# Projections and attention in one block: the first quad's loads and first max tiles between the last batch's projection groups

## What is computed

```python
x = x + tanh(g_xattn[0]) * attention(layernorm(x), ctx, mask, mask, Wq, bq, Wk, bk, Wv, bv)
x = x + tanh(g_ffn[0]) * ffn_fp8(layernorm(x), W2, scale, scale1)
# attention: q = Wq x + bq; k = Wk c + bk; v = Wv c + bv, 16 heads of 32 channels
#   dot = mask * (q k / sqrt(32)) - (1 - mask) * 1e6 ; out = (softmax(dot) * mask) v
```

## Time and profile before

| | us |
|---|---|
| median of 3 runs | 2610.9 (2610.55 to 2611.96) |
| the profiled execution | 2608.16 |
| its span in the trace | 2606.3 |
| PE busy in the span | 2505.3 (96%) |
| DVE busy | 1978.2 (76%) |
| POOL busy | 1653.4 (63%) |
| ACT busy | 1393.0 (53%) |

### The profile page before, as it was taken

The page is one execution under the profiler, slowest core; times in us unless marked ns, Lnnn a source line. Parts: engine busy times, 40 slices in busy tenths (PEclk is TensorE's granted clock), DMA queues, the critical chain, the costliest instruction groups (busy, mean ns, idle before and its releaser), DMA issues.

```text
span 2606.3 us, 40566 instructions
## 1 busy us (share of the span) xinstructions
PE 2505.3 (96%) x13169; PEld 1385.0 (53%) x13169; DVE 1978.2 (76%) x3251; ACT 1393.0 (53%) x2606; POOL 1653.4 (63%) x1265
## 2 busy tenths in 40 slices
PE   5999999978999999999999999999999999999995
PEld 4888888864444444444444444444444444444441
DVE  5766666637788888888888888888888888888863
ACT  2333333322666666666666666666666666666662
POOL 1333333422777777777777777777777777777774
PEclk8999999996999999999999999999999999999997
DMA  6666666655334444444444444344444444444411
GB/s 213 229 236 236 234 234 233 237 171 96 76 80 89 88 96 91 98 103 99 103 98 93 91 93 93 88 88 88 96 91 96 102 100 102 100 94 92 91 37 49
DMA packets 242040, 314.48 MB, mean 121 GB/s; under 512 B 75033, under 2 KB 142681, under 8 KB 241857
## 3 DMA queue, kind: packets, MB, share of 16 engines
q1 hardware_dynamic: 229712, 274.20, 42.2%
q10 hardware_dynamic: 12144, 38.02, 4.1%
HBM read 200.09 MB, written 102.11 MB: 116 GB/s over the span
## 4 chain that ended last, share of the span: by engine, by line
PE 66%; DVE 6%; issue 3%; POOL 1%; DMA 1%; ACT 0%; SPq 0%; DVEq 0%; POOLq 0%; ACTq 0%
PE s_bank L690 19%; PE o_bank L716 18%; PE x_bank L703 16%; PE d_bank L727 7%; PE x_bank L742 5%; DVE part_max L849 4%; POOL pair_sum L942 1%; PE x_bank L734 1%; DVE y L103 1%; DMA q_st<-qx_scr 0%; DVE isnan L102 0%; POOL y L951 0%; ACT probs L785 0%; DMA inv_b<-inv_scr 0%; DVE neg_max L863 0%
## 5 line engine op out<-in xcount | busy, mean ns | idle before, releaser
L942 POOL TENSOR_TENSOR pair_sum<-probs 128x512 f32<-128x512 f32 x1024 | 1284.2, 1288 | 472.0 <-ACT probs L785 472.0
L849 DVE TENSOR_REDUCE part_max<-x_bank 128x1 f32<-128x512 f32 x2048 | 1280.9, 683 | 355.6 <-PE x_bank L703 348.8
L785 ACT ACTIVATE probs<-s_bank 128x512 f32<-128x512 f32 x2048 | 1071.5, 604 | 662.3 <-PE s_bank L690 655.0
L690 PE MATMUL s_bank<-q_st,k_st 100*128 100x512 f32 x2048 | 876.5, 430 | 4.7 <-ACT probs L785 4.7
L703 PE MATMUL x_bank<-k_st,q_st 98*128 98x512 f32 x2048 | 823.6, 406 | 24.8 <-DMA q_st<-qx_scr 21.5
L690 PEld LDWEIGHTS s_bank<-q_st,k_st 100*128 100x128 f32 x2048 | 387.1, 189 | 511.5 <-issue 263.2
L716 PE MATMUL o_bank<-probs,v_t 128*32 128x512 f32 x4096 | 545.5, 605 | 0.0
L703 PEld LDWEIGHTS x_bank<-k_st,q_st 98*128 98x128 f32 x2048 | 393.1, 192 | 141.8 <-DMA q_st<-qx_scr 22.0
L727 PE MATMUL d_bank<-pair_sum,ones 128*32 128x512 f32 x2048 | 266.6, 592 | 2.8 <-POOL pair_sum L942 2.8
L322 POOL TENSOR_TENSOR stage_lo<-stage,stage_hi 128x512 fp32r<-128x512 f32 x128 | 187.3, 1487 | 120.7 <-ACT stage_hi L392 120.1
L392 ACT ACTIVATE stage_hi<-stage 128x512 fp32r<-128x512 f32 x128 | 79.8, 632 | 190.2 <-DVE stage L476 142.9
(11 more groups left out here) (96 smaller groups left out, 2018.9 us busy)
## 6 DMA issues: line engine op xcount, KB each, us to landing
k_st<-k_scr SPq DMA_DIRECT2D x96, 512.0 KB
q_st<-q_scr SPq DMA_DIRECT2D x192, 256.0 KB
c_raw<-in_ctx_dram ACTq DMA_DIRECT2D x32, 512.0 KB, 6.7
x_raw<-in_x_dram ACTq DMA_DIRECT2D x32, 512.0 KB, 6.2
k_scr<-stage_hi SPq DMA_DIRECT2D x64, 256.0 KB, 2.4
k_scr<-stage_lo SPq DMA_DIRECT2D x64, 256.0 KB, 2.6
v_scr<-stage SPq DMA_DIRECT2D x64, 256.0 KB, 2.7
q_scr<-stage_hi SPq DMA_DIRECT2D x64, 256.0 KB, 2.1
```

Source lines behind the costliest of these rows:

```text
L690: nc.tensor.matmul(s_bank_of(n, k)[:, :], k_st[p][0:KS, h, j * P:(j + 1) * P], q_st[p][0:KS, th, h, :], start=True, stop=True).then_inc(sc ...
L785: nc.scalar.activation(probs[:, c % PR, h, :], s_bank_of(n, k)[:, :], ACT.Exp).then_inc(exp_done, 1)
L849: nc.vector.tensor_reduce(part_max[:, th, sh, at:at + 1], x_bank_of(n, "tile", k)[:, :], AX, ALU.max).then_inc(max_done, 2)
L942: nc.gpsimd.tensor_tensor(pair_sum[:, r % 2, h], probs[:, a, h], probs[:, a + 1, h], ALU.add).then_inc(pair_done, 1)
```

## The change

The projections and the attention become one block. All PSUM is one set of eight banks: attention's s banks are banks 0 to 2, o and d are 3 and 4, x are 5 to 7. Small tiles and the stage buffers get places of their own; `k_st[0]` and `q_st[0]` lie where `c_raw` and `x_raw` were, and `k_st[1]`, `q_st[1]` over the projection weights.

- Only in the last batch, PE's groups go round five banks (0 to 4), so group g waits for group g - 5.
- SP issues `stack_k(0, 0)` at the start of the last batch, after `clo_done`; `stack_q(0, 0)` before the stores of group 4, after `xlo_done`; `load_v(0, 0)` before those of group 16; `set_max(0, 0, 0)` before those of group 20; and `stack_k(1, 1)`, `stack_q(1, 1)` before those of group 22, after the last group is done.
- From group 12 PE runs one slot of period -1 after each group's four channel blocks: slots 19 to 63, which hold the 45 max tiles of quad 0 and one turn of the maxima. DVE takes three maxima, evacuates the group, takes the fourth.
- DVE's last `round_w2` moves from between v groups 11 and 12 to before v group 8.
- The unused `ident_b` and its copy go; the semaphore waits at the block's end go, and `wait_stored` has SP wait for a batch's stores at each fourth quad.

```diff
+            G_MAX = 12
+            def slots_of_group(g):
+                first = XLEAD + 4 * (g - G_MAX)
+                return range(first, min(first + 4, NSLOT)) if g >= G_MAX else range(0)
+            def bank_of_group(g, more):
+                return bank[g % NB] if more else bank[g % NB_LAST]
...
 # SP
                     def batch(b, more):
+                        if not more:
+                            sp.wait_ge(clo_done, B * CB)
+                            stack_k(0, 0)
                         for g in range(G):
+                            if not more and g == 4:
+                                sp.wait_ge(xlo_done, B * CB)
+                                stack_q(0, 0)
+                            if not more and g == GK + GV:
+                                sp.wait_ge(w2_done, B)
+                                load_v(0, 0)
+                            if not more and g == G - 4:
+                                set_max(0, 0, 0)
+                            if not more and g == G - 2:
+                                sp.wait_ge(group_done, B * G)
+                                stack_k(1, 1)
+                                stack_q(1, 1)
...
 # PE
+                            back = NB if more or g < NB_LAST else NB_LAST
+                            if counted(b * G + g + 1 - back):
+                                pe.wait_ge(evacuated, b * G + g + 1 - back)
...
+                                if not more and cb < len(slots_of_group(g)):
+                                    slot(-1, 1, slots_of_group(g)[cb])
...
 # DVE
+                        for g in range(GK // 2, GK + GV // 2 if more else GK):
+                            evacuate(b, g, more)
+                        round_w2(b)
+                        if more:
...
+                        else:
+                            for g in range(GK, GK + GV):
+                                max_and_evacuate(b, g)
...
+                    def max_and_evacuate(b, g):
+                        slots = slots_of_group(g)
+                        for k in slots[:CB - 1]:
+                            slot(-1, 1, k)
+                        evacuate(b, g, False)
+                        for k in slots[CB - 1:]:
+                            slot(-1, 1, k)
...
-                for n in range(-2, NQ + 2):
+                for n in range(NQ + 2):
```

More of the change, by code:

```diff
@@ new lines, in flamingo_gated_layer @@
+        inv_c = sb("inv_c", [P, HALF // 32], F32)
+        tm_c = sb("tm_c", [P, TH, HALF // 32], F32)
+        st2 = sb("st2", [P, 2, 6], F32)
+        mv2 = sb("mv2", [P, 2], F32)
+        ve2 = sb("ve2", [P, 1], F32)
+        rs2 = sb("rs2", [P, 1], F32)
+        rss = sb("rss", [P, 2], F32)
+        nb2 = sb("nb2", [P, 1], F32)
+        bank = [pb(f"bank{i}", [P, HALF], F32) for i in range(8)]
+        c_loaded = [sem(f"c_loaded{i}") for i in range(CB)]
+        x_loaded = [sem(f"x_loaded{i}") for i in range(CB)]
@@ L118, in flamingo_gated_layer @@
-            x_raw = sb("x_raw", [P, CB, T], F32, st)
-            c_loaded = [sem(f"c_loaded{i}", st) for i in range(CB)]
-            x_loaded = [sem(f"x_loaded{i}", st) for i in range(CB)]
             with ExitStack() as su:
@@ L606, in flamingo_gated_layer @@
[L606 to L613 removed]
+            v_t = [sb(f"v_t{i}", [P, SJ, P], F32, at) for i in range(2)]
+            s_bank, o_bank, d_bank, x_bank = bank[0:3], bank[3], bank[4], bank[5:8]
@@ new lines, in flamingo_gated_layer, with run_batches @@
+            NB, NB_LAST = len(bank), 5
+            GK = CB * 2
+            GV = SJ
+            G = 2 * GK + GV
+            G_MAX = 12
[4 more added lines that the diff above has]
+                return bank[g % NB] if more else bank[g % NB_LAST]
+            def run_batches(eng, batch):
+                batch(0, True)
+                if B > 2:
+                    with eng.Fori(1, B - 1) as b:
+                        batch(b, True)
+                batch(B - 1, False)
@@ L1080 @@
+                            slot(n, p, k)
+                    low_ctx(0)
+                    statistics(0)
+                    normalize(0)
+                    run_batches(dve, batch)
+                    run_periods(period)
 _INS = ['x', 'ctx_2048', 'mask_Bx1x2048_fk1', 'g_xattn', 'g_ffn', 'L0_xattn_Wq', 'L0_xattn_bq', 'L0_xattn_Wk',
```

1044 lines of the change are left out of this document (508 added, 536 removed).

## The result

| | before | changed |
|---|---|---|
| median of 4 runs each, one chip, us | 2611.43 (2610.55 to 2612.59) | 2564.81 (2563.17 to 2569.08) |
| ratio, 95% interval | | 0.9824 (0.9807 to 0.9841) |
| the profiled execution, us | 2608.16 | 2563.17 |
| its span, us | 2606.3 | 2561.4 |

The changed kernel is 46.6 us faster. The forecast was 36.2 us, and the time lies 3.2 us under the low end of the range.

The account below looks back on a forecast made before the run. PE, 96% busy, bounds the kernel; gains lie in the 50.6 us gap. With waits of 3.0 and 2.5 us, slot 19 moves from 638.92 to 602.75, 36.2 us less: 2610.9 to 2574.7 us, range 2568 to 2586.

Parts of the forecast that it names:

- the first sentence of the new timeline: Seven batches before the last: same instructions, so the last batch's first matmul stays at 506.82, a change of 0.
- the rival on the new places: Attention: new banks and SBUF addresses stretch PE's steady pace, paid 32 times; then, say, 2618 us; chance 0.05.
- the gap closes: Between projections and scores: the 50.6 us gap goes, 45 max tiles cost 10.6 us among the projections, first score near 587.
- the queue: SP's queue, last batch: stack loads delay stores, DVE stands 4.3 us at `evacuate(12)`, PE loses 3.0 us (bounds 0 to 8).
- the first rival: SP's queue: loads hold stores longer, `evacuate(12)` stalls over 8 us and the clock falls; 2582 to 2596 us, chance 0.11.
- the forecast's own case: Whole run: 0 to 8 us for the queue, 0 to 5 for quad 1; 2569 to 2582 us, chance 0.72.
- quad 1's stack: Slot 19, after the first score: stack issued at 584.25, tile 0 can start at 599.75, PE waits 2.5 us.
- DVE has room: Last batch's groups: four maxima and one evacuation take 3.1 us of a 3.7 us group, 0.6 us to spare.
- The rounding of W2: DVE, last batch: 6.0 us, moved before group 8, about 529.7 to 535.7, costing nothing.
- attention keeps its pace: Attention behind the gap: unchanged, with PE at least 61.3 us busy in 62 us stretches.

Follow-up runs that it names:

- lay_only_c: The kernel before with y8 copied plainly, not transposed, and the projections' SBUF tiles at the changed kernel's offsets; schedule as before: 2598.9 us, ratio 0.9954.
- after_pad64_c: The changed kernel with y8 copied plainly, not transposed, and 64 bytes of padding between weights and split inputs (and ahead of `v_t`): 2570.6 us.
- before_c: The kernel before with one edit, the transposing transfer of y8 made a plain copy of the same size: 2609.86 us, ratio 0.9994.
- after_c: The changed kernel with one edit, the transposing transfer of y8 made a plain copy: 2565.39 us, ratio 0.9823.
- late_half_c: From after_c, the second half of quad 0's q stack is issued before group 16 instead of group 4: 2557.6 us, ratio 0.9798.

## Why the prediction was wrong, point by point

**The step that failed** is the first sentence of the new timeline: "The first matmul of the last batch stays at 506.82: the seven batches before are the same instructions." It came at 498.71. The instructions are the same, their operands' addresses are not, and `lay_only_c` shows that these alone give it. The change moves every tile of the projections, and the diff says so; the text took from that only a rival by which new places might slow attention. The projections' pitch of 0.230 was taken as what the engine does with 512 columns, and the rival on the new places even leaned on it ("at one pace of 0.230 us"). It is a mean of two paces, 0.229 for q and 0.233 for v, and that groups of one shape differ was the sign, readable before, that something beside the shape sets it. This term was 0 and should have been -8.1 between these two traces. With attention's 3.7 us, whose cause is open, it carries the time out of the range.

**Right: the gap closes.** The first score follows the last projection at its pitch, the clock no longer falls at the end of the projections, and the 45 max tiles ride along. The stretch took 83.16 us where 80.4 were forecast. At about the pace that the forecast was made for, `after_pad64_c` has 80.9, in one run.

**Right in place, undersized: the queue.** The wait is DVE's at group 12, ended by a v store, with the loads in order ahead of it. DVE waits 4.66 us (forecast 4.3), PE 4.23 (forecast 3.0), and 1.5 us go to the clock. At the old pace it was 2.67 and 2.4 (`after_pad64_c`), without the clock: what this term is over the forecast comes from the pace again, and the forecast was somewhat high for its own pace. That the two nearly meet at 4.3 and 4.66 us is luck. The mechanism of the first rival, a pause that takes the clock down, came true within the forecast's own case: a pause of 4.2 us was enough, where the text charged it only from 8.

**Right: quad 1's stack.** From the first score to its first max tile 15.55 us, as forecast (599.75 - 584.2), with 1.75 us of waiting instead of 2.5.

**Right: DVE has room.** Beside the pause, PE waits for a maximum once more before 620, for 0.3 us. The rounding of W2 took longer than the 6.0 us that were charged. Its steps on DVE's timeline of the changed kernel, and POOL beside them:

```profile
524.83 2.20 DVE L98 TENSOR_TENSOR w2q<-w2f,w2big 128x1024 bf16<-128x1024 f32 x1
527.06 1.40 DVE L101 TENSOR_SCALAR w2nan<-w2q 128x1024 bf16<-128x1024 bf16 x1
528.50 1.66 DVE L102 TENSOR_TENSOR w2q<-w2q,w2nan 128x1024 bf16<-128x1024 bf16 x1
...
523.68 7.63 POOL L469 TENSOR_TENSOR stage_lo<-stage,stage_hi 128x512 fp32r<-128x512 f32 x4 [6.31 <-ACT stage_hi L697]
```

The same three steps took 1.22, 0.43 and 0.69 us before, when POOL was idle, and they take 1.23, 0.43 and 0.69 in the changed kernel one batch earlier (470.57 to 472.99), where POOL is idle too. In the last batch POOL subtracts beside them, and the whole takes 8.9 us. It stayed under cover. The Trainium skill, page "SBUF — State Buffer", section "SBUF: two separate sides", names the port that GpSimd and the vector engine share as the place where compute engines meet; the two batches fit that. But the port itself shows in no trace, and no run here took POOL's work away from these steps, so this cause is argued and not shown.

**Nearly right: attention keeps its pace.** Forecast as unchanged, it is 3.7 us or 0.2% shorter over 31 quads, too little to be seen in stretches of 62 us. Two of them, of the changed kernel (before: the earlier trace rows, 61.35 and 61.66):

```profile
840.00:902.00 62.00, 61.50 (x348) 29.57 (x347) 50.96 (x89) 38.31 (x76) 46.34 (x37) 1.00 0.43 96
2300.00:2362.00 62.00, 61.67 (x344) 29.96 (x342) 50.93 (x88) 38.50 (x76) 46.34 (x37) 1.00 0.42 93
```

`k_st` and `q_st` have a distance of 0 modulo 256 bytes in both kernels, which fits.

The profiled execution in one line: forecast 2572.0, minus 8.1 for the addresses, plus 2.8 for the last batch (1.2 more pause, 1.5 clock, 0.1 of small terms), minus 3.7 for attention and plus 0.3 around it, gives 2563.3; measured 2563.17. Without the addresses and attention's 3.7 us the step from the forecast to the measurement would be 3 us, and inside the range.

## What to carry to other kernels

A change that moves tiles changes the pace of code that it doesn't touch: before "the same instructions take the same time", compare the addresses of stationary and moving operands, and if two kinds of matmul of one shape have two pitches, try a padding first. It is one line, and here it is worth 10 us (2599 to 2600 instead of 2610). A load that nobody needs for 20 us should not stand in a queue ahead of a store that frees a buffer: give it a later place or another queue. And where one engine gets faster, work out again the waits that are set by transfers, since those grow by what it gained.

## What the runs showed of the hardware

- An fp32r matmul of 512 columns with its own weight load takes 0.2267 us from start to start where both operands lie alike modulo 256 bytes in a partition, and 0.229 to 0.233 us where they lie 64 or 128 bytes apart; at 64 the pace changes from group to group at the same addresses (21.97 or 22.40 us for 96 in `before_c`).
- Three steps of DVE on 128x1024 took 2.20, 1.40 and 1.66 us beside POOL's subtractions and 1.23, 0.43 and 0.69 us without them, in one trace (changed kernel).
- PE's clock fell to 1.2 GHz after pauses of 4.2 us (changed kernel, 8 matmuls at the lower pace, 1.5 us lost), 2.35 (`after_c`) and 1.78 (`after_pad64_c`), and did not after pauses of 2.4 (`after_pad64_c`), 1.87 (`late_half_c`) and 1.75 (changed kernel).
- With the DMA engines full, stack loads alone moved 202 to 238 GB/s, and the same loads mixed with stores from another queue 363.
- Copying y8 plainly or turning it in the transfer makes no measurable difference to the time of this kernel (0.9984 to 1.0004).
